# First attention: the values' transposes wait for an earlier count, the copies' wait stands one product later, and the queries' low half is made ahead of the masks

## The reference

```python
qkv = inputs @ W_qkv                      # inputs 8 x 512 x 256
q = 32 heads of 64;  k, v = 16 heads of 64, each repeated for two query heads
scores = einsum('bhqd,bhkd->bhqk', q, k) / sqrt(64) + slope[h] * (key position - query position)
attn = softmax(where(query >= key, scores, -inf))
out = einsum('bhqk,bhkd->bhqd', attn, v)  ->  reshape  ->  out @ W_out
```

## Time and profile before

| | before |
|---|---|
| median of 3 runs | 3567.09 us (3566.45 to 3567.75) |
| profiled execution, its own time | 3567.49 us |
| its span, first to last instruction | 3565.7 us |
| stretch of the 128 bodies | 70.3 to 1592 us of the span |
| PE busy in the span | 3262.8 us, 92% |
| DVE, ACT, POOL busy | 66%, 58%, 33% |

### The profile page before, as it was taken

How to read it: one execution, slowest core, us unless ns; L and a number is a source line. 1 busy time by engine, 2 the same in 40 slices (tenths; PEclk the granted TensorE clock), 3 DMA queues, 4 the chain that set the end, 5 groups by cost and what they waited for, 6 DMA issues and landing times. The chain is left out here.

```text
span 3565.7 us, 74087 instructions
## 1 busy us (share of the span) xinstructions
PE 3262.8 (92%) x22696; PEld 2398.6 (67%) x22696; DVE 2341.9 (66%) x6849; ACT 2081.7 (58%) x4943; POOL 1186.7 (33%) x1818
## 2 busy tenths in 40 slices
PE   5999999999999999998999997969999964999995
PEld 3666666666666666667888884546666654888885
DVE  5777777777777777776666664546666635666665
ACT  4777677777777677775555553216656630555553
POOL 4333333333333333333333330033132102243442
PEclk9999999999999999999999998979999976999998
DMA  3221222222222222225334332111111133554545
GB/s 92 52 56 42 57 51 57 51 55 54 52 57 51 57 51 57 51 46 166 124 125 134 125 129 77 42 47 26 27 31 27 27 101 104 168 125 129 137 123 159
DMA packets 175949, 280.44 MB, mean 79 GB/s; under 512 B 32851, under 2 KB 117587, under 8 KB 175827
## 3 DMA queue, kind: packets, MB, share of 16 engines
q1 hardware_dynamic: 161234, 258.94, 25.4%
q0 software_dynamic: 14592, 19.93, 3.4%
HBM read 159.79 MB, written 41.16 MB: 56 GB/s over the span
## 5 line engine op out<-in xcount | busy, mean ns | idle before, releaser
L767 POOL TENSOR_SCALAR at_p<-at_p,at_recip 128x128 f32<-128x128 f32 (+3 forms) x1028 | 536.5, 536 | 958.0 <-DVE at_recip L900 958.0
L815 ACT ACTIVATE at_p<-at_p,at_nmax 128x128 f32<-128x128 f32 (+3 forms) x1030 | 573.5, 557 | 383.5 <-DVE at_nmax L894 380.2
L894 DVE CUSTOM_DVE_ANT_0 at_p<-at_s_ps,at_bias 128x128 f32<-128x128 f32 (+3 forms) x1030 | 498.1, 484 | 385.8 <-PE at_s_ps L1029 379.5
L1029 PE MATMUL at_s_ps<-at_k_twice,at_q 64*128 64x128 f32 (+3 forms) x3090 | 418.5, 362 | 54.0 <-DVE acc L912 49.8
L1029 PEld LDWEIGHTS at_s_ps<-at_k_twice,at_q 64*128 64x128 f32 x3090 | 245.7, 185 | 260.6 <-issue 246.0
L1860 DVE CUSTOM_DVE_ANT_0 aa_a_ps<-aa_a_ps,aa_hidden 128x128 f32<-128x128 f32 (+3 forms) x512 | 247.1, 507 | 176.2 <-PE aa_a_ps L2024 173.2
L1050 PE MATMUL at_o_ps<-at_pT,at_v 128*64 128x512 f32 (+3 forms) x2064 | 315.1, 446 | 0.0
L1760 ACT ACTIVATE aa_pT<-aa_b_ps 128x512 f32<-128x512 f32 (+1 forms) x384 | 196.7, 529 | 179.5 <-PE aa_b_ps L2042 176.6
L526 DVE SCALAR_TENSOR_TENSOR nw_hl<-nw_h,nw_coef_now,nw_hh 128x512 fp32r<-128x512 f32 x192 | 150.4, 783 | 164.4 <-ACT nw_hh L454 164.4
L449 ACT ACTIVATE nw_h<-nw_h_ps,nw_b 128x512 f32<-128x512 f32 x192 | 132.2, 689 | 211.0 <-PE nw_h_ps L553 210.6
L905 DVE COPY at_pT<-at_t_ps 128x128 f32<-128x128 f32 (+3 forms) x512 | 248.1, 484 | 0.0
(11 more groups left out here) (317 smaller groups left out, 7947.0 us busy)
## 6 DMA issues: line engine op xcount, KB each, us to landing
at_k_twice<-at_k_parts SPq DMA_DIRECT2D x260, 256.0 KB, 3.6
w_raw<-in_w_dram SPq DMA_DIRECT2D x57, 768.0 KB
nw_w_raw<-in_w_all_dram SPq DMA_DIRECT2D x26, 1024.0 KB, 5.0
nw_w_raw<-in_w_all_dram SPq DMA_DIRECT2D x52, 512.0 KB, 6.6
nw_xh<-xh_dram SPq DMA_DIRECT2D x10, 512.0 KB, 4.2
nw_xl<-xl_dram SPq DMA_DIRECT2D x10, 512.0 KB, 4.9
at_w_raw<-in_w_heads_dram SPq DMA_DIRECT2D x18, 256.0 KB, 4.4
nw_x<-in_x_dram SPq DMA_DIRECT2D x9, 512.0 KB, 5.9
```

The lines of the kernel that those rows point to most:

```text
L767: pool.tensor_scalar(p, p, recip[:, u:u + 1], 1.0, ALU.mult, ALU.mult).then_inc(scaled, 1)
L815: act.activation(p_sb[:, u, 0:N], p_sb[:, u, 0:N], ACT.Exp, bias=nmax[:, u:u + 1], scale=-1.0, accum_out=total[:, u:u + 1]).then_inc(exped, 1)
L894: dve.tensor_tensor_reduce(out=p_sb[:, u, 0:N], in0=s_ps[u % 2][:, 0:N], in1=bias[:, u % 2, S - N:S], scale=1.0, scalar=BIG, op0=ALU.add, ...
L1029: ins = pe.matmul(s_ps[h][:, 0:N], qst[par][rows, q, at], k_twice[par][rows, k, 0:N], start=(i == 0), stop=(i == 2))
```

## The change

PE asks for `proj_out` of `v_count(t + 1) - 4` = 5t + 2 ahead of product 1: two readings fewer, the last one asked for being the previous body's `k_rest`, which reads the bank that `turn_v` then overwrites. `turned_out(t - 1)` stands ahead of product 2, behind `turnable(t, 0)`. One wait for `proj_out` of 4 is added ahead of the loops, since in body 0 the count of 2 would not cover `k_rest`. On DVE `q_rest` stands ahead of both masks of qt = 0 instead of behind them.

```diff
@@ DVE, body
+                    if qt == 0:
+                        q_rest(t + 1, 1 - par)
                     mask(n, u)
                     invert(*soon(t, qt))
                     mask(n, u + 1)
-                    if qt == 0:
-                        q_rest(t + 1, 1 - par)
                     turn_out(t, qt, par)
@@ PE, score
                     if i == 2 and late is not None:
                         turnable(*late)
+                        if late[1] == 0:
+                            turned_out(late[0] + (-1))
@@ PE, body
                     if qt == 0:
-                        def between():
-                            values_free(t + 1, v_count(t + 1) + (-2))
-                            turned_out(t + (-1))
-                        score(n, n_par, u, between, (t, qt))
+                        score(n, n_par, u, lambda: values_free(t + 1, v_count(t + 1) + (-4)), (t, qt))
@@ PE, ahead of the loops
+            pe.wait_ge(proj_out, 4)
             with pe.Fori(0, KVH) as j:
```

## The result

The changed kernel takes 3473.2 us (median of 4 runs, 3470.2 to 3475.2), the kernel before beside it 3567.4 us (3566.5 to 3568.9): a ratio of 0.9735, 95% interval 0.9718 to 0.9752. That is 94 us less.

A forecast was written before the change was run, and what follows sets the result against it. PE's stream was taken to bound the 128 bodies, with a wait for DVE's L912 in each. 127 bodies gaining 0.62 + 0.02 = 0.64 us make 81 us: 3567.1 - 81 = 3486 us, range 3474 to 3516.

The forecast's parts named there:

- What bounds the kernel, and the mechanism: In the 128 bodies PE is busy 97%; its repeated wait for DVE's L912 ahead of a score goes with the earlier count.
- 1.61 - 0.99 = 0.62 us a body: 512-column score: 1.61 us as read, less 0.99 undisturbed (with 0.20 for the last step), gives 0.62 us gained a body.
- I take 0.02: Last part of weigh: its weights need no release once q_rest is early; 0 to 0.07 us a body, taken as 0.02.
- The range: Whole kernel: 3474 to 3516 us, the first case's 3476 to 3493 and nearly all of the second case.
- its 0.65 for the score: Score's part of the upper bound of 0.72 us a body: 1.61 - 0.96, with the smaller step; 0.07 for weigh added.
- It would become the stall that takes the removed one's place: q_rest left behind the masks, with PE 0.62 us earlier: its exactly met wait in weigh would become the new stall.
- the move is what lets the gain through: Putting q_rest ahead of both masks on DVE was claimed necessary for the 0.62 us gain to come through.
- The same paragraph's figures for the kernel with the move: DVE with q_rest moved: q_rest from 707.6, its successor at 708.2, masks unmoved, the 128-column copy starting 709.55 instead of 710.18.
- The copies' wait: Moved ahead of product 2 of the 512-column score: just met, thinnest margin; zero cost taken, up to 0.2 us if missed.
- What is late next: PE's next score, 128 columns: second mask good for 709.95, margin 0.2 us; copy good for 710.15, product 2 due near 710.4.
- The rival on the other side: Slower, 5%: a late take_q delays q_rest and both masks, eating the gain from 0.84 us on; 3587 us at 1.0 us.

The follow-up runs named there:

- late_count: The changed kernel with the old, later count (wait for DVE's last add_out) put back ahead of product 1, everything else as changed: 3555.2 us.
- low_half_only: The kernel before with only q_rest moved ahead of both masks, the waits as they were: 3558.5 us.
- the second measurement: The changed kernel run again unaltered, beside the kernel before: 3470.2 us, ratio 0.9733.
- count_only: The changed kernel with q_rest back in its old place behind both masks: 3479.4 us.
- copies_first: The changed kernel with the copies' wait back ahead of product 1; the earlier count and the moved q_rest stay: 3472.6 us.
- two_spares: The changed kernel with two unread DVE reductions of 512 columns between q_rest and the first mask: 3597.5 us.
- spare_reduce: The changed kernel with one unread DVE reduction of 384 columns between q_rest and the first mask: 3505.0 us.

## Why the prediction was right in kind and too small

**What bounds the kernel, and the mechanism: right.** The wait for L912 was the stall, the earlier count took it away, and no other wait took its place. late_count and low_half_only show that the count alone carries it: with the old count 82.5 and 84.4 of the 91.2 us are lost (1513.1 and 1515.0 less 1430.6), with the early count and nothing else of weight 85.2 us are won (1521.8 - 1436.6).

**"1.61 - 0.99 = 0.62 us a body": the step that was mis-sized.** It measured 0.695 us, for two reasons. The score now takes 0.96 us; the step to 512 columns is 0.16 to 0.17 us, like the one ahead of it, and not 0.20. And 1.61 us was one body read, where bodies alternate between two kinds. The timeline of before, one body on:

```profile
718.47 0.50 PE L1029 MATMUL at_s_ps<-at_k_twice,at_q 64*128 64x512 f32 x2
719.35 0.82 PE L1029 MATMUL at_s_ps<-at_k_twice,at_q 64*128 64x512 f32 x4 [0.38 <-DVE acc L912]
```

Here the score takes from 718.47 to 720.17, 1.70 us: behind the release, products 1 and 2 need 0.82 us and not 0.73. In the changed kernel the next body's score is again 0.96 us:

```profile
712.76 0.96 PE L1031 MATMUL at_s_ps<-at_k_twice,at_q 64*128 64x512 f32 x6
```

The mean of the two is 1.655 us, and 1.655 - 0.96 = 0.695 us, 0.075 more than the term. The bodies of before alternate like this all along; over 125 of them the mean is 1.66 us, and 0.96 in the changed kernel. I read the two kinds as the sequencer's. Ahead of product 2 the longer kind has one wait instruction more (L1014). The first row is of the shorter kind, the other two are of the longer:

```profile
L1015 PEldq EVENT_SEMAPHORE  x1: 51/51/51, 707.5 to 707.5; - x1
...
L1014 PEldq EVENT_SEMAPHORE  x1: 51/51/51, 719.5 to 719.5; - x1
L1015 PEldq ALU_OP  x1: 32/32/32, 719.6 to 719.6; - x1
```

Behind a release such an instruction would count, as in late_count. In the changed kernel, where nothing holds the sequencer, both kinds take 0.96 us. That reading was not tested by itself.

**"I take 0.02" for the last part of weigh:** it measured 0.04 to 0.05 us (4.8 to 6.8 us by the two experiments), within the 0 to 0.07 given.

**The rest of the sum.** 0.695 + 0.05 = 0.745 us against 0.718 measured, so some 0.03 us a body are given back elsewhere. They are the 0.04 us by which the other stretches between scores became longer; why they did, no run shows. In microseconds, between the two profiled executions: 81.3 predicted, 9.9 more in the bodies (127 x 0.078), 0.4 ahead of them and 3.9 behind them are the 95.5 by which the spans differ (3565.7 - 3470.2); the medians differ by 94.

**The range.** The time lies 0.8 us below it, and 3.8 us in the second measurement (3470.2 us). The bodies alone are just inside: 0.718 us each, and the range was made from 0.72. That is luck in part, since its 0.65 for the score was too small and the 0.04 us given back was not in it. What the range had no term for is the second attention. By the profiles it differs by 3.9 us with PE's clock, and that part isn't the change's doing as far as the runs show.

**"It would become the stall that takes the removed one's place": wrong.** This was said of q_rest without its move, and "the move is what lets the gain through". count_only shows the contrary. I had shifted PE and left DVE standing, though DVE idled 1.28 us for exactly the score that came sooner. The same paragraph's figures for the kernel with the move nearly hold: q_rest right behind ACT's take_q, its successor 0.6 us later, the copy 0.72 us sooner where 0.63 was forecast (2.95 us behind the score's start, before 3.67).

**The copies' wait: right to take zero, for too weak a reason.** The margin was called the thinnest. copies_first asks for the copies a whole product sooner, and lost nothing.

**What is late next: the wrong one of two.** 0.2 us were given for the mask and 0.25 for the copies (710.15 against 710.4). The copies have 0.24 us, and they are the thinner margin; the mask has 0.45. The prediction took 0.35 us from the mask's end to PE, as it had read behind add_out, and that release takes 0.04 us. The rival on the other side said that the gain is eaten from 0.84 us of lateness on. By two_spares, 1.19 us late and 0.94 us a body slower, the gain of 0.72 us is used up at 0.96 us; the mechanism is real, but nothing in the changed kernel is late by more than the margin.

## What to carry to other kernels

A wait on a counter asks for everything that was counted up to it. Where PE waits for an operation that reads another buffer than the one about to be written, look which earlier count would do; here two fewer are worth 2.4% of the kernel, and reordering the waits nothing.

When a stall is removed, move along everything that waited for what comes sooner, before looking for the next stall. An engine that idled for it is early too; only work that hangs on something else (here ACT's take_q) stays where it was.

Take a loop's cost from at least two rounds, or from the stretch divided by its count. And measure a stall by start to start: the marked idle time was 0.39 us, what it cost 0.67 (85.2 us in 127 bodies, by count_only).

## What the runs showed of the hardware

A release reaches PE at very different prices. In spare_reduce the second mask's last instruction ends at 706.08 and the weights that wait for it are loaded at 706.12, 0.04 us later; in the kernel before, the add_out ends at 707.01 and product 1's weights are loaded at 707.36, 0.35 us later. The first wait sits on the weight load itself, the second on an instruction of the sequencer with others behind it. late_count and low_half_only show it for the same wait: 0.12 us with one, 0.36 with the other. The Trainium skill ("Perfetto Trace Analysis", section "Identifying Dependency Chains") says that an instruction that waits for several engines may have EventSemaphore instructions put in front of it; that agrees with the order shown ahead of the prediction. By these traces such instructions are free as long as their counts are met early, and cost some 0.25 to 0.3 us when they stand between a release and the product.
